# A transformer block on one core: later transposes in the second chunk's preparation, layer-norm statistics moved into the feed-forward, and other waits for the last pair of heads

## The reference

```python
def block(x):
    x = x + attn(layernorm(x))
    return x + ffn(layernorm(x))

def attn(x):            # 16 heads, d = 32
    Q, K, V = proj(Wq, bq), proj(Wk, bk), proj(Wv, bv)
    Q = Q * cos + rotate_half(Q) * sin          # the same for K
    scores = Q @ K.T / sqrt(d)                  # causal: -inf above the diagonal
    return softmax(scores) @ V  ->  (B, S, H) @ Wo.T + bo

def ffn(x):             # gate_w, up_w: (1408, 512), down_w: (512, 1408), ternary
    g = x @ gate_w.T * gate_s
    u = x @ up_w.T * up_s
    return ((silu(g) * u) @ down_w.T) * down_s
```

## Time and profile before

| what | value |
|---|---|
| time, median of 3 runs | 780.58 us (780.42 to 780.86) |
| the profiled execution | 777.7 us, span 776.0 us |
| mean granted TensorE clock | 0.991 of full speed |
| PE busy | 741.8 us, 96% of the span |
| DVE busy | 437.7 us, 56% |
| ACT busy | 301.7 us, 39% |
| POOL busy | 246.1 us, 32% |
| stage A / B / C1 / C2 (from the chain of work, rounded) | 0 to 163 / 163 to 473 / 473 to 519 / 519 to 776 us |

### The profile page before, as it was taken

One profiled execution on the slowest core, in us unless ns is written; L12 is line 12 of the kernel. 1 busy time (PEld: TensorE's weight loads), 2 busy tenths in 40 slices (PEclk: granted clock), 3 DMA queues, 4 the chain that ended last, 5 costly groups with the idle time before them and its releaser, 6 DMA issues.

```text
span 776.0 us, 10609 instructions
## 1 busy us (share of the span) xinstructions
PE 741.8 (96%) x3539; PEld 541.2 (70%) x3539; DVE 437.7 (56%) x1103; ACT 301.7 (39%) x639; POOL 246.1 (32%) x224
## 2 busy tenths in 40 slices
PE   7979999989999999999999989998999999999996
PEld 6768888765555555555555536886888888888885
DVE  6948593988777777777777726793125114215112
ACT  3231313246555555555555563213232223223221
POOL 0713352501114141414141426921223123223223
PEclk9989999999999999999999999999999999999998
DMA  8294649645556565656665564570001001001001
GB/s 288 74 361 175 247 163 301 248 149 162 153 154 180 154 182 161 179 160 178 165 181 161 133 188 116 231 311 0 1 0 55 1 1 54 0 0 54 1 1 56
DMA packets 54318, 104.39 MB, mean 135 GB/s; under 512 B 14820, under 2 KB 18404, under 8 KB 53748
## 3 DMA queue, kind: packets, MB, share of 16 engines
q1 hardware_dynamic: 54264, 103.72, 43.0%
HBM read 69.62 MB, written 38.21 MB: 139 GB/s over the span
## 4 chain that ended last, share of the span: by engine, by line
PE 86%; DVE 5%; ACT 3%; issue 3%; DMA 1%; POOL 1%; SPq 0%; ACTq 0%; DVEq 0%; POOLq 0%
PE ps L1078 39%; PE ps L1196 17%; PE ps L1272 10%; PE ps L1103 9%; PE ps L1177 9%; PE ps L1070 2%; ACT p L664 1%; ACT o_raw L671 1%; DVE xn L769 1%; DMA w_st<-in_wk 1%; DMA q_st<-neg_max_T 0%; ACT neg_max_T L678 0%; DVE stats L992 0%; DVE osin L877 0%; DMA x_st<-in_x 0%
## 5 line engine op out<-in xcount | busy, mean ns | idle before, releaser
L664 ACT ACTIVATE p<-ps 128x384 f32<-128x384 f32 (+3 forms) x384 | 161.9, 488 | 123.9 <-PE ps L1177 123.6
L826 DVE CUSTOM_DVE_ANT_0 masked<-ps,mask_qk 128x512 bf16<-128x512 f32 (+1 forms) x240 | 115.4, 503 | 74.3 <-PE ps L1103 71.7
L1177 PE MATMUL ps<-q_st,k_st 99*128 99x384 f32 (+2 forms) x384 | 134.6, 369 | 6.8 <-ACT p L664 6.6
L1196 PE MATMUL ps<-p,v_slot 128*64 128x512 f32 (+3 forms) x768 | 137.5, 493 | 2.1 <-ACT p L664 1.4
L1103 PE MATMUL ps<-k_st,q_st 96*128 96x512 f32 (+2 forms) x384 | 130.9, 362 | 1.4 <-DVE row_max L826 1.2
L1037 DVE SCALAR_TENSOR_TENSOR hid<-ps,us_sb,silu 128x512 f32<-128x512 f32 x44 | 33.0, 751 | 170.0 <-PE ps L1078 166.7
L576 POOL TENSOR_TENSOR hid_lo<-hid,hid_hi 128x512 fp32r<-128x512 f32 x44 | 56.8, 1291 | 176.8 <-ACT hid_hi L744 176.8
L545 POOL TENSOR_SCALAR_AFFINE_SELECT p<-p 128x512 f32<-128x512 f32 x64 | 40.8, 637 | 212.2 <-ACT p L664 212.2
L1196 PEld LDWEIGHTS ps<-p,v_slot 128*64 128x64 f32 x768 | 52.4, 136 | 74.7 <-issue 62.6
L1103 PEld LDWEIGHTS ps<-k_st,q_st 96*128 96x128 f32 x384 | 72.2, 189 | 31.3 <-issue 21.9
L1177 PEld LDWEIGHTS ps<-q_st,k_st 99*128 99x128 f32 x384 | 72.3, 189 | 26.3 <-ACT p L664 16.0
(11 more groups left out here) (113 smaller groups left out, 1073.6 us busy)
## 6 DMA issues: line engine op xcount, KB each, us to landing
qk_scratch<-st_hi SPq DMA_DIRECT2D x32, 512.0 KB, 3.8
q_st<-qk_scratch SPq DMA_DIRECT2D x32, 384.0 KB, 3.9
k_st<-qk_scratch SPq DMA_DIRECT2D x32, 384.0 KB, 4.9
flag_st<-in_ffn SPq DMA_DIRECT2D x32, 264.0 KB, 2.8
ffn_copy<-in_ffn SPq DMA_DIRECT2D x32, 264.0 KB, 3.4
qk_scratch<-st_lo SPq DMA_DIRECT2D x16, 512.0 KB, 4.0
o_T<-o_raw SPq DMA_DIRECT2D x32, 128.0 KB, 4.0
rec_l<-rec_rows SPq DMA_DIRECT2D x32, 128.0 KB, 3.4
```

The source lines that it names most:

```text
L664: act.activation(p32[:, at:at + q0 + w - keep], ps[:, ST_BANK + i % ST_RING, keep - q0:w], ACT.Exp, scale=SCALE).then_inc(exp_done, 1)
L826: ins = dve.tensor_tensor_reduce((masked_a if u < 2 else masked)[:, s_before(i) % 2, col:col + kept], scores, mask_qk[:, 512 - kept:512], ...
L1177: pe.matmul(ps[:, ST_BANK + i % ST_RING, 0:w], k_st[0:K_ALL, slot, kt * P:(kt + 1) * P], q_st[0:K_ALL, slot, q0:q0 + w], start=True, stop= ...
L1196: ins = pe.matmul(ps[VW * a:VW * (a + 1), O_BANK, q0 - 512 * half:512], v_slot[:, slot, kt, :], p32[:, at:at + n], start=(kt == 0), stop=( ...
```

## The change

Five edits:

1. **Stage A, chunk 0 only.** The 16 transposes of chunk 1's tokens were 8 behind value tile 0 and 8 behind value tile 1. They are now all behind value tile 2 (`next_tiles`). ScalarE's order follows: `values(0)`, `values(1)`, `high(3)`, `values(2)`, four `transposed_hi`, `values(3)`. The other chunks keep the old order.
2. **Stage A, chunk 0.** VectorE's `weight_lo(3)` moves from ahead of `rotate(0)` to behind it.
3. **Last pair of heads.** Its half 1 goes to bank 4 instead of bank 7 and waits for the last exponential instead of the copy of half 0.
4. **Every pair.** Group 0 waits for the exponentials up to piece 8 of the second head, not for all 12.
5. **Statistics of chunks 2 and 3.** Moments, square roots and reciprocals for the residuals of the last two chunks move from ahead of the feed-forward to behind `hid` i = 4 of its chunk 0 (`LATE_STATS = 4`) on VectorE, and behind `hid_hi` i = 4 on ScalarE. `tokens(c)` waits for its own chunk's reciprocals.

```diff
+LATE_STATS = 4
+        def o_bank(u, half):
+            return ST_BANK if (u, half) == (PAIRS - 1, 1) else O_BANK
+        def next_tiles(c, j):
+            if c == 0:
+                return range(TJ) if j == 2 else ()
+            return (2 * j, 2 * j + 1) if j < 2 else ()
...
# ScalarE, stage A
-                    for half in range(2):
-                        values(half)
-                        transposed_hi(c + 1, 2 * half)
-                        transposed_hi(c + 1, 2 * half + 1)
-                    high(3)
-                    values(2)
-                    values(3)
+                    for j in range(TJ):
+                        values(j)
+                        for k in next_tiles(c, j):
+                            transposed_hi(c + 1, k)
+                        if j == 1:
+                            high(3)
...
# ScalarE, C1 and C2
-                if c != N_CH - 2:
-                    if c == N_CH - 1:
-                        std_of(N_CH + c - 1)
+                if c < N_CH - 2:
                     std_of(N_CH + c)
...
                     act.copy(hid_hi[:, i % 3, :], hid[:, i % 2, :]).then_inc(hid_hi_done, 1)
+                    if c == 0 and i == LATE_STATS:
+                        std_of(2 * N_CH - 2)
+                        std_of(2 * N_CH - 1)
...
# VectorE
-            weight_lo(3)
...
                 rotate(0)
+                if c == 0:
+                    weight_lo(3)
...
             def tokens(c):
+                dve.wait_ge(ln_rstd, N_CH + c + 2)
...
-            chunk_moments(N_CH - 2)
-            ln_reciprocal(2 * N_CH - 2)
-            dve.wait_ge(ln_moments, 2 * N_CH)
-            for j in range(TJ - 1):
-                tile_stats(N_CH - 1, j)
-            chunk_moments(N_CH - 1)
-            ln_reciprocal(2 * N_CH - 1)
...
-            dve.wait_ge(ln_rstd, 2 * N_CH + 1)
...
+                    if c == 0 and i == LATE_STATS:
+                        chunk_moments(N_CH - 2)
+                        ln_reciprocal(2 * N_CH - 2)
+                        dve.wait_ge(ln_moments, 2 * N_CH)
+                        for j in range(TJ - 1):
+                            tile_stats(N_CH - 1, j)
+                        chunk_moments(N_CH - 1)
+                        ln_reciprocal(2 * N_CH - 1)
...
# TensorE
-                    elif j < 2:
-                        if j == 0:
-                            pe.wait_ge(ln_done, c + 3)
-                        for k in (2 * j, 2 * j + 1):
+                    elif next_tiles(c, j):
+                        pe.wait_ge(ln_done, c + 3)
+                        for k in next_tiles(c, j):
...
-                    pe.wait_ge(exp_done, NPC * (2 * u + 2))
+                    pe.wait_ge(exp_done, NPC * (2 * u + 1) + P_LOW + 1)
...
-                    if kt == 0 and 2 * u + half > 0:
+                    if kt == 0 and (u, half) == (PAIRS - 1, 1):
+                        pe.wait_ge(exp_done, NPC * HEADS)
+                    elif kt == 0 and 2 * u + half > 0:
                         pe.wait_ge(o_evac, 2 * u + half)
```

More of the change, by code:

```diff
@@ L670, in evacuate_half @@
                     act.wait_ge(o_moved[u % 2], 64 * (u // 2))
-                act.copy(o_raw[:, u % 2, half * 512:(half + 1) * 512], ps[:, O_BANK, :]).then_inc(o_evac, 1)
+                act.copy(o_raw[:, u % 2, half * 512:(half + 1) * 512], ps[:, o_bank(u, half), :]).then_inc(o_evac, 1)
             def next_max(t):
@@ L1195, in output_products @@
                         at = slot * P_SIZE + P_OFF[kt] + q0 - P * kt
-                        ins = pe.matmul(ps[VW * a:VW * (a + 1), O_BANK, q0 - 512 * half:512], v_slot[:, slot, kt, :],
+                        ins = pe.matmul(ps[VW * a:VW * (a + 1), o_bank(u, half), q0 - 512 * half:512], v_slot[:, slot, kt, :],
                                         p32[:, at:at + n], start=(kt == 0), stop=((half, kt) in PV_LAST), skip_group_check=True)
```

## The result

| kernel | median | lowest to highest | executions | profiled execution | span |
|---|---|---|---|---|---|
| before | 780.5 us | 778.93 to 780.86 | 4 | 777.7 us | 776.0 us |
| after | 774.59 us | 773.56 to 775.32 | 4 | 774.45 us | 772.7 us |

The ratio after/before is 0.9927, 95% interval 0.9909 to 0.9945: 5.9 us faster (interval 4.3 to 7.1). 773.0 was forecast, with 770.0 to 776.5 around it. The two profiled executions differ by 3.25 us only, where the sum said 7.7. Both gaps have to be explained: 1.6 us between forecast and median, 4.4 us between forecast and trace.

What follows compares the result with a forecast made beforehand. The prediction took TensorE, 86% of the chain of waits, as the bound. Gains of 2.1 (stage A), 1.2 (end of stage B) and 4.4 us (feed-forward) sum to 7.7, from median 780.58 to 773.0; range 770.0 to 776.5.

Steps and rivals of the forecast that it cites:

- Stage A, the rotation: Chunk 0: rotation runs from 17.4 to 20.2, weight in its shadow until 21.4; waits of 1.31 and 0.47 us go.
- Stage A, the transposes: The 4.64 us gap before them goes; a 4.9 us wait comes before chunk 1, which starts at 51.2, 4.3 us earlier.
- The rival in which the stores don't move: Stage A: ScalarE waits until 50.1 as before, 0.9 us lost instead of 2.1 won; 776.0 us, 13%.
- The low clock behind the gap: Stage A, behind the new gap before chunk 1: TensorE's clock falls and costs 2.2 us.
- The rival without it: Stage A: the new gap does not slow the clock, so 2.2 us more are won; 770.8 us, 15%.
- Stage A together: Edits 1 and 2: 4.3 us won up to chunk 1, less 2.2 of low clock, net 2.1 us gained.
- The end of stage B: Last pair: 0.45 us from group 0's wait, 0.68 from half 1, some 0.05 of hand-over; together 1.2 us gained.
- The start of the feed-forward: Edit 5: the 3.43 us gap and 1.79 of low clock go, 5.2 us; `down(5)` waits 0.8; net 4.4 us.
- from SiLU to `down` 3.98 pass: Feed-forward start: 3.98 us from SiLU at 522.1 put `hid_lo` at 526.1, with TensorE free at 526.19, so no wait.
- the 1.79 us for the low clock: Feed-forward start: eight `down` matmuls took 3.60 us behind the gap, later ones 1.81; this 1.79 us loss goes.
- The rival of longer statistics: Feed-forward: table switches take twice 1.28 us, TensorE waits 3.4 us and pays 1.8 more; 777.4 us, 5%.

Runs made afterwards that it cites:

- second trace of the changed kernel: The changed kernel, unchanged, run again for its time and another trace: median 774.9 us, profiled execution 772.3 us.
- stage A alone: The kernel before with edits 1 and 2 alone: 779.74 us, ratio 0.9972.
- split statistics: The changed kernel with chunk 2's late statistics behind `hid` i = 3 and chunk 3's behind i = 6: 773.2 us in one look.
- Copies first: The changed kernel with `high(3)` of chunk 0 behind the four copies of transposed tokens on ScalarE: 770.78 us, ratio 0.9878.
- late statistics alone: The kernel before with edit 5 alone: 777.54 us, ratio 0.9945.
- copies before both: The changed kernel with `high(2)` and `high(3)` of chunk 0 behind ScalarE's four token copies, `low(2)` behind the transposed tokens' low parts: 774.46 us, ratio 0.9921.
- early tokens: Copies before both, with the load of chunk 2's tokens ahead of the stores of p = 2 and 3: 766.26 us, ratio 0.9817.
- all together: Early tokens and split statistics in one kernel: 767.53 us, ratio 0.9835.
- rotation alone: The kernel before with edit 2 alone: 784.28 us in one look.

## Why the prediction was right, and where not

**Stage A, the rotation: right as a mechanism, mis-sized by a collision and by the clock.** The prediction let the weight run "in its shadow until 21.4" and priced nothing for what starts beside it. In the second trace of the changed kernel this is what happened, within 0.3 us: weight done at 21.62, `value_weight_lo(5)` at 32.92 (32.7 forecast), chunk 1 at 51.42 (51.2). In the first trace the weight met GpSimd's addition and lost 1.0 us: 22.82, 34.13, 52.63. The Trainium skill (SBUF — State Buffer, Who interferes with whom) says that a VectorE instruction with two inputs in SBUF and a GpSimd instruction that reads SBUF exclude each other for a whole instruction, and the one issued first goes first; both traces agree (2.27 and 1.29, 1.23 and 2.35 us). The other cause is the clock ahead of the rotation. With a mean clock of 0.83 from 10 to 20 us it started at 18.88 (stage A alone) and 19.19 (split statistics), not at 17.5, and chunk 1 came at 52.30 and 52.87. The first product's end at 17.4 was read from one trace with a clock of 1.00 there; only 5 of the 14 traces have that.

**Stage A, the transposes: right.** No gap ahead of them (42.48), TensorE done at 47.1, `high(2)`, `high(3)`, one value copy and four token copies in the order and with the durations of the sum, and a gap of 5.51 and 5.04 us (4.9 forecast). Copies first shows that `high(3)` was the cause. The rival in which the stores don't move is out: they landed 1.1 us earlier in the first trace and 2.2 in the second (`high(3)` at 49.10 and 47.89, against 50.1).

**The low clock behind the gap: right.** From the start of chunk 1 to its transposes 24.49 us pass before (55.48 to 79.97) and 26.60 after (52.63 to 79.23), 2.1 us of loss for 2.2 forecast. The second trace lost 1.9 us (26.40). The rival without it is out: the clock fell in every trace with this gap.

**Stage A together: 2.1 forecast, about 1.6 measured.** A comes on average at 165.28 in the four traces without both edits and with the old code there (165.03, 165.75, 165.91, 164.44) and at 163.72 in the four with them (164.30, 162.87, 163.55, 164.16). Each group spreads over some 1.5 us, so 1.6 is good to about 1 us and the 2.1 forecast is not refuted. The second trace of the changed kernel, in which the weight came first, is 2.16 us ahead of the trace before, as forecast.

**The end of stage B: the sum exact, its terms less so.** 1.2 forecast, 1.21 measured. The first part of the pair came 0.31 us earlier after its score pieces (5.01 to 4.70 us) where 0.45 was forecast: TensorE starts 0.14 us behind the end of the copy of bank 7 (465.15 to 465.29), while the sum took none. From there to the output projection 0.91 us were won (8.80 to 7.89), not 0.73. The two misses cancel, which is luck.

**The start of the feed-forward: 4.4 forecast, 3.7 measured.** The table load and SiLU went as worked out: SiLU at 522.51 where the sum, moved by the 0.41 us by which the output projection starts later, says 522.5. Three terms were off. The first is "from SiLU to `down` 3.98 pass": it was 4.35, so `down(0)` waits 0.36 us where the sum had none. The second is the 1.79 us for the low clock. The prediction compared eight `down` products behind a wait (3.60) with eight in full flow (1.81), but behind the wait of 0.50 us the chain after has 2.06 us for eight at full clock. From `down(0)` to `down(2)` 12.54 us pass before and 11.00 after, so the low clock had cost 1.54. The third went the other way: `down(5)` came 6.10 us behind `down(4)` instead of 5.44, 0.66 us lost where 0.8 was forecast (0.50 of it shows as wait). Another 0.34 us are lost behind `down(5)` (217.52 to 217.86); this stretch varies from 217.10 to 218.23 between the traces, so they may be chance. The chain after names the 0.35 us that are new in the first term, on VectorE between two waits of one `hid`:

```profile
523.24 0.05 DVEq L1040
523.29 0.40 issue
523.69 0.05 DVEq L1041
```

Before, the same place has 0.05 of issue. The late statistics alone have 0.40 there as well, so it belongs to this edit. The first wait is for this SiLU, which ended at 523.21. The second is for a count of 0 (`hid_lo_done`, no `hid` before this one), so it has nothing to wait for; why it is taken up late wasn't tried and stays open. The rows again show no drain such as the Trainium skill (ScalarE: Activation LUTs, What ACT_TABLE_LOAD costs) states for each switch of table: the two switches that the edit adds have their function 0.02 us behind the load (544.92 and 546.22) and 0.01 us behind it (549.86 and 551.15). The rival of longer statistics is out.

**The trace's shortfall.** Of the 4.4 us between sum and trace, stage A makes 1.4 (2.1 - 0.73), the feed-forward 0.7 (4.4 - 3.71), and stage B 2.35: A to B should have become 1.2 shorter and became 1.14 longer. 1.7 us of it are the row maxima's late transfers. They are not the whole cause: the second trace of the changed kernel takes 307.97 us from A to B, 1.4 more than forecast, with 0.7 us of such waits. Do edits 1 and 2 cause the late transfers? In the six traces without both edits they cost 0 (three times), 0.3, 0.5 and 0.7 us; in the six with both and up to copies before both, 0.7 to 2.4; but with an even earlier stage A (early tokens, all together) only 0.7 and 0.4. Nothing here changed these transfers alone, so the cause stays open. The forecast had counted on the same stage B, and this is the term of the sum that failed in both traces.

**The median.** The parts measured across traces give 1.6 + 1.2 + 3.7 = 6.5 us; 5.9 and, the second time, 4.8 between medians (ratio 0.9927 both times, 4.3 to 7.1) leave up to 1 or 2 us for stage B. That the profiled pair shows only 3.3 has a second reason: the profiled execution of before was a good one, 2.8 us under the median of 780.5, while that of after lies at its median, and the sum rightly was applied to the median.

## What to carry to other kernels

When a gap is removed, follow the engine that releases the next one through its own queue: here the wait stood behind ScalarE's `high(3)`, then behind a load on SyncE, and only with all three orders changed did TensorE run through, for 13 to 14 us instead of 5 to 6. A gap costs its length and the clock behind it, but closing it pays only up to the next wait: in copies first the gap shrank by 3.65 us and the low clock went, and the first score piece came only 2.65 us earlier. A sum read from one trace also takes over that trace's clock: edit 2 pays with a clock of 1.00 ahead of the rotation and cost about 1 us in the one run with 0.66. Judge a part of a change by a stretch between two instructions that it alone can move (12.60 against 13.80 us here), since the whole time varies by more than the part.

## What the hardware showed beside this

The clock also fell without one long gap. In stage A alone, the late statistics alone and the rotation alone it fell at the start of stage B, where TensorE waits often and briefly. The late statistics, windows of 2 us:

```profile
176.00:178.00 2.00, 1.48 (x9) 1.26 (x9) 2.00 (x8) 1.32 (x4) 0.43 (x1) 1.00 0.57 139
178.00:180.00 2.00, 1.54 (x4) 1.17 (x4) 1.62 (x9) 0.83 (x3) 1.19 (x3) 0.66 0.85 273
180.00:182.00 2.00, 2.00 (x6) 1.32 (x4) 1.84 (x8) 1.55 (x3) 0.00 (x0) 0.50 0.89 283
```

The longest wait of TensorE between 160 and 190 us there is 0.95 us; before it is 0.72. Over 172 to 188 us the mean clock was 0.79 in these three traces and 1.00 in the others. 0.21 of 16 us is 3.4 us, and A to B takes 311.2 to 313.5 us in the three against 307.3 to 309.8 in the others. That can be a good part of the 10 us over which executions of one kernel spread. No edit is common to these three kernels; what decides on the fall wasn't tried.
